# Layer-norm moments taken in the stage that writes the tile, and the input loaded in four transfers

## The reference

```python
def _layernorm(x, axis=-1, eps=1e-05):
    m = jnp.mean(x, axis=axis, keepdims=True)
    v = jnp.var(x, axis=axis, keepdims=True)
    return (x - m) / jnp.sqrt(v + eps)
...
    x = x + _L0_attn_ref(_layernorm(x, axis=-1), ...)
    x = x + _L0_ffn_ref(_layernorm(x, axis=-1), ...)
    ...
    x = x + _L3_ffn_ref(_layernorm(x, axis=-1), ...)
    return x
```

## Time and profile before

| what | value |
|---|---|
| median of 3 runs | 4477.09 us (4474.5 to 4481.69) |
| the profiled execution's own time | 4479.81 us |
| its span in the trace | 4478.1 us |
| TensorE (PE) busy | 3905.1 us, 87% |
| VectorE (DVE) busy | 2310.9 us, 52% |
| ScalarE (ACT) busy | 1725.0 us, 39% |
| GpSimd (POOL) busy | 1224.5 us, 27% |
| mean granted TensorE clock | 0.921 |

### The profile page before, as it was taken

One profiled execution on the slowest core, in us unless ns is written; L12 is line 12 of the kernel. 1 busy time (PEld: TensorE's weight loads), 2 busy tenths in 40 slices (PEclk: granted clock), 3 DMA queues, 4 the chain that ended last, 5 costly groups with the idle time before them and its releaser, 6 DMA issues. The chain is left out here.

```text
span 4478.1 us, 105382 instructions
## 1 busy us (share of the span) xinstructions
PE 3905.1 (87%) x45357; PEld 2429.4 (54%) x45424; DVE 2310.9 (52%) x4298; ACT 1725.0 (39%) x2719; POOL 1224.5 (27%) x1771
## 2 busy tenths in 40 slices
PE   7887759999995685799899779999999999999869
PEld 3333555555543373477555545656666666666636
DVE  5764243444555124344433256776677776766541
ACT  2345222112112010455211145666556665555532
POOL 2000120000003314311000035555555555554511
PEclk9999759999996797899899889999999999999879
DMA  1000000000003062100100000000000000000000
GB/s 51 1 1 1 30 0 26 11 2 10 11 3 111 26 195 62 40 1 1 57 1 0 8 8 9 9 11 11 9 10 9 9 9 9 9 9 9 6 15 19
DMA packets 38396, 92.00 MB, mean 21 GB/s; under 512 B 7422, under 2 KB 27679, under 8 KB 34426
## 3 DMA queue, kind: packets, MB, share of 16 engines
q1 hardware_dynamic: 27578, 69.54, 4.6%
q0 software_dynamic: 6144, 11.62, 0.9%
q10 hardware_dynamic: 4224, 4.19, 0.3%
HBM read 70.05 MB, written 20.45 MB: 20 GB/s over the span
## 5 line engine op out<-in xcount | busy, mean ns | idle before, releaser
L2725 PE MATMUL ps<-h_normT,h_w 128*128 128x512 f32 (+1 forms) x1008 | 425.0, 526 | 28.7 <-DVE h_xx L3312 21.6
L3246 DVE SCALAR_TENSOR_TENSOR h_cv<-h_raw,h_cw,h_cv 128x1023 f32<-128x1023 f32 (+2 forms) x288 | 389.2, 1361 | 20.0 <-ACT h_cv L3073 18.9
L3390 DVE SCALAR_TENSOR_TENSOR h_st<-h_st,d_gcs,ps 128x64 f32<-128x64 f32 x448 | 123.5, 276 | 345.7 <-PE ps L3021 345.6
L3072 ACT ACTIVATE h_raw<-ps 128x512 f32<-128x512 f32 x192 | 114.2, 595 | 404.1 <-PE ps L2725 403.3
L2725 PEld LDWEIGHTS ps<-h_normT,h_w 128*128 128x128 f32 x1008 | 165.3, 190 | 134.3 <-issue 116.8
L472 ACT ACTIVATE a_prob<-ps 128x1024 f32<-128x1024 f32 (+1 forms) x192 | 154.6, 811 | 192.8 <-PE ps L384 104.6
L956 PE MATMUL ps<-a_probT,a_v 128*128 128x512 f32 x512 | 227.6, 603 | 0.8 <-DVE a_probT L1094 0.8
L2622 POOL TENSOR_TENSOR h_gm<-h_gm,h_tmp 128x15 f32<-128x15 f32 (+7 forms) x480 | 217.3, 453 | 37.6
L2187 PE MATMUL ps<-h_normT,e_wgu 128*128 128x512 f32 (+1 forms) x448 | 204.1, 599 | 5.2 <-DMA e_wd<-in_e_wd 4.0
L1243 POOL MEMSET r_zero<- 128x2048 f32 x1 | 1.8, 1807 | 728.2 <-POOLq L54 728.2
L3021 PEld LDWEIGHTS ps<-h_st,h_mT 64*64 64x64 f32 x1792 | 90.7, 133 | 199.1 <-issue 195.0
(11 more groups left out here) (537 smaller groups left out, 9336.6 us busy)
## 6 DMA issues: line engine op xcount, KB each, us to landing
m_wgu<-in_m_wgu SPq DMA_DIRECT2D x8, 1408.0 KB
h_w<-in_d_w SPq DMA_DIRECT2D x48, 128.0 KB
m_wd<-in_m_wd SPq DMA_DIRECT2D x8, 704.0 KB
m_rows_in<-r_zero SPq DMA_DIRECT2D x4, 1024.0 KB
e_xe<-m_rows_in SPq DMA_DIRECT2D x8, 512.0 KB
m_rows_out<-e_y ACTq DMA_DIRECT2D x8, 512.0 KB
e_wgu<-in_e_wgu SPq DMA_DIRECT2D x1, 3520.0 KB
a_t_raw<-in_t_w SPq DMA_DIRECT2D x4, 768.0 KB
```

Source lines behind the costliest of these rows:

```text
L2725: last = pe.matmul(ps[:, PROJ[m], lo:hi], w[:, kind, k, :], hT[:, k, b * S + tb * BANK + lo:b * S + tb * BANK + hi], start=(k == 0), stop= ...
L3246: dve.scalar_tensor_tensor(out=d, in0=raw[:, kind, 0:S - back], scalar=tap(pr, kind, TAPS3 - 1 - back), in1=d, op0=ALU.mult, op1=ALU.add). ...
```

## The change

`core` gets a stats tile that lives for the whole run. `bn_stats` leaves `layer_norm`, which starts with the 16 `bn_aggr`. Each stage that adds the last term of a tile runs `bn_stats` (the helper `measure`) on that tile: as a rule one step behind, that is after the next tile's add has been issued, behind a wait for the tile's own add, and for the last tile (or the last two) after the loop. For x as loaded, `bn_stats` runs in `load_and_constants`, where VectorE measures four tiles behind each of four transfers of 512 KB; SyncE no longer waits there. In `add_rows` the add of r = 0 gets the wait for the add before it, too. In `thought0` the scaled adds get a semaphore, and the first half is measured between `moments_own(1)` and `finish(1)`.

```diff
+        self.stats = sb("x_stats", [P, NT, 6])
+def measure(core, dve, t):
+    return dve.bn_stats(core.stats[:, t, :], core.x[:, t, :])
...load_and_constants
-            sp.dma_start(core.x[:], core.dram["x"]).then_inc(loaded, 16)
-            sp.wait_ge(loaded, 16)
+            for i in range(PIECES):
+                t0, t1 = piece(i).start, piece(i).stop
+                sp.dma_start(core.x[:, t0:t1, :], core.dram["x"][:, t0:t1, :]).then_inc(loaded[i], 16)
+        @block.vector
+        def _(dve):
+            for i in range(PIECES):
+                dve.wait_ge(loaded[i], 16)
+                for t in piece(i):
+                    measure(core, dve, t)
...layer_norm
-            for t in range(NT):
-                dve.bn_stats(stats[:, t, :], core.x[:, t, :]).then_inc(stats_ready, 1)
             for t in range(NT):
-                dve.wait_ge(stats_ready, t + 1)
-                dve.bn_aggr(mv[:, t, :], stats[:, t, :]).then_inc(mv_ready, 1)
+                dve.bn_aggr(mv[:, t, :], core.stats[:, t, :]).then_inc(mv_ready, 1)
...attention0 (experts2 the same)
                 dve.tensor_tensor(core.x[:, t, :], ps[:, t % 8, 0:H], core.x[:, t, :], ALU.add).then_inc(x_added, 1)
+                if t >= 1:
+                    dve.wait_ge(x_added, t)
+                    measure(core, dve, t - 1)
+            dve.wait_ge(x_added, NT)
+            measure(core, dve, NT - 1)
...thought0
-                                             op0=ALU.mult, op1=ALU.add)
+                                             op0=ALU.mult, op1=ALU.add).then_inc(x_done, 1)
             moments_own(1)
+            for n in range(HALF):
+                dve.wait_ge(x_done, n + 1)
+                measure(core, dve, n)
             finish(1)
+            for n in range(HALF, NT):
+                dve.wait_ge(x_done, n + 1)
+                measure(core, dve, n)
...attention1
                 dve.tensor_tensor(xs, ps[:, u % 4, :].rearrange("p (t n) -> p t n", t=2), xs, ALU.add).then_inc(x_added, 1)
+                if u >= 1:
+                    dve.wait_ge(x_added, u)
+                    measure(core, dve, 2 * u - 2)
+                    measure(core, dve, 2 * u - 1)
+            dve.wait_ge(x_added, NT // 2)
+            measure(core, dve, NT - 2)
+            measure(core, dve, NT - 1)
...combine1, add_rows
-                    if r >= 1:
+                    if n >= 1:
                         dve.wait_ge(added, n)
-                    elif t >= NT // 2:
+                    if r == 0 and t >= NT // 2:
                         dve.wait_ge(x_added, t - NT // 2 + 1)
                     dve.scalar_tensor_tensor(...).then_inc(added, 1)
+                    if r == 0 and t >= 1:
+                        measure(core, dve, t - 1)
+            dve.wait_ge(added, NT * TOP1)
+            measure(core, dve, NT - 1)
...scan_mlp2
             def residuals(i):
+                if i >= 3:
+                    dve.wait_ge(x_added, i - 1)
+                    measure(core, dve, order[i - 3])
                 dve.wait_ge(out_p, i)
...
+            dve.wait_ge(x_added, NT + 1)
+            measure(core, dve, order[NT - 2])
+            measure(core, dve, order[NT - 1])
...heads3
             def end(t):
                 for g in range(2):
                     gate(t, g)
+                dve.wait_ge(xa, 4 * UNITS3)
                 for k in range(4):
                     add(t, k)
+                    for j in range(2):
+                        measure(core, dve, 2 * k + j)
+                    if k >= 1:
+                        dve.wait_ge(xa, 4 * UNITS3 + k)
+                        for j in range(2):
+                            measure(core, dve, NQ + 2 * k - 2 + j)
+                dve.wait_ge(xa, 4 * UNITS3 + 4)
+                for j in range(2):
+                    measure(core, dve, NT - 2 + j)
```

More of the change, by code:

```diff
@@ L71, in load_and_constants @@
     with Phase(core, "init") as ph:
-        loaded, filled, shaped = ph.sem("loaded"), ph.sem("filled"), ph.sem("shaped")
+        filled, shaped = ph.sem("filled"), ph.sem("shaped")
+        PIECES = 4
+        loaded = [ph.sem(f"loaded{i}") for i in range(PIECES)]
         block = ph.block()
+        piece = lambda i: range(i * NT // PIECES, (i + 1) * NT // PIECES)
         @block.sync
         def _(sp):
-            sp.dma_start(core.x[:], core.dram["x"]).then_inc(loaded, 16)
-            sp.wait_ge(loaded, 16)
+            for i in range(PIECES):
[7 more added lines that the diff above has]
+                    measure(core, dve, t)
         @block.gpsimd
@@ L107, in layer_norm @@
     with Phase(core, tag) as ph:
-        stats = ph.sb("stats", [P, NT, 6])
         mv = ph.sb("mean_var", [P, NT, 2])
@@ L111, in layer_norm @@
         rstd = ph.sb("rstd", [P, NT])
-        stats_ready, mv_ready, std_ready, rstd_ready = (ph.sem(n) for n in ("stats", "mv", "std", "rstd"))
+        mv_ready, std_ready, rstd_ready = (ph.sem(n) for n in ("mv", "std", "rstd"))
         h_ready, turned, copied = ph.sem("h"), ph.sem("turned"), ph.sem("copied")
@@ L662, in thought0 @@
         (load, g_done, gated, summed, squared, var_sum, std_ready, t_ready, lin, a_ready, gelu, dlin, rep_ready, bc_done,
-         bc_ready, dve_own, pool_own, o_ready, stat, aggr, so_ready, norm, load_first, sig, biased) = (ph.sem(n) for n in (
+         bc_ready, dve_own, pool_own, o_ready, stat, aggr, so_ready, norm, load_first, sig, biased, x_done) = (ph.sem(n) for n in (
              "load", "g_done", "gated", "summed", "squared", "var_sum", "std", "t", "lin", "a", "gelu", "dlin", "rep", "bc_done",
-             "bc", "dve", "pool", "o", "stat", "aggr", "so", "norm", "load_first", "sig", "biased"))
+             "bc", "dve", "pool", "o", "stat", "aggr", "so", "norm", "load_first", "sig", "biased", "x_done"))
         block = ph.block()
```

## The result

The changed kernel takes 4460.7 us (median of 10 runs, 4447.2 to 4475.1) against 4477.1 of the kernel before (10 runs, 4472.8 to 4488.5). The ratio is 0.996, 95% interval 0.9947 to 0.9974: 16.4 us faster, 12 to 24 by the interval. The forecast was 4451.8.

A forecast was written before the change was run, and what follows sets the result against it. TensorE, busy 87% of 4478.1 us, was taken to idle at eight layer-norm starts awaiting the moments, 42.0 us in all. Eight edge gains sum to 25.3 us, taking the median from 4477.1 to 4451.8; range 4445 to 4461.

The forecast's parts named there:

- The removed group: At the start of all eight layer norms: 16 bn_stats, 5.25 us each time with other engines waiting, 42.0 us in all.
- the table: ScalarE's square-root table load in six of eight layer norms becomes late next, costing about 0.1 us each.
- The load: Input in four transfers: only the last quarter's four bn_stats exposed, 1.39 us; gain 3.8 us.
- Rival A: First 10 us: each quarter of the load pays its own landing in turn, 8.4 us lost, time 4460.2; 5%.
- attention0, mixer, experts2: Edges after these stages: VectorE idles enough to hide all but the last two measures; gain 4.5 us each.
- thought0 and attention1: Edges where VectorE has no gap: all 16 measures come back in full; gains 0 and -0.1 us.
- combine1: Edge after combine1: 15 measures hide in waits and the sixteenth too; gain 5.2 us, or 4.7 if wrong.
- heads3: Edge after heads3: add 2 is 0.25 us late, 2.25 us exposed in all; gain 2.9 us.
- Rival B: TensorE's clock in the layer norms' transposes: 3.7 us more gained (4448.1), 10%, or 5.9 lost (4457.7), 5%.
- C: Moments hide almost nowhere: attention0, combine1, mixer and experts2 give back all 16, 6.6 us remain, time 4470.5; 4%.
- D: Measures behind waits hold VectorE some 0.6 us each, exposed at all 129: 35 us slower, 4512; 1%.

The follow-up runs named there:

- e5: The changed kernel unaltered, measured again in a second session beside the kernel before: 4451.9 us against 4477.6.
- e8: Changed kernel with eight input transfers, the mixer's doubled measure gone, heads3's first sequence measured ahead of the gates: 4448.6 us, ratio to before 0.9938.
- e6: The changed kernel with the load as one transfer instead of four: 4454.9 us.
- e12: The changed kernel with every moved bn_stats issued twice, the first into a spare tile: 4418.5 us against 4423.9 of the kernel before.
- e1: The kernel before with the persistent stats tile allocated but unused: 4435.5 us against 4434.7, ratio 0.9995.
- e11: Changed kernel, still four transfers, the mixer's doubled measure gone, heads3's first sequence measured ahead of the gates: 4396.1 us against 4423.9 of the kernel before.
- e10: The changed kernel cut to load, layer norms 4 and 5, mixer, experts2 and store: 748.6 us against 754.5 of the kernel before cut likewise.

## Why the prediction was right, and where it was not

**The forecast** of 25.3 us stands as a sum of mechanisms: 26.8 by the edges of one profile, 25.7 in e5's session. The first session's 16.4 us just stay in the range (4460.7 against an upper end of 4461), and its interval does not hold 25.3. That 4460.7 stayed inside is luck, and so is e5's median, 0.1 us from the forecast, with runs of one kernel that far apart. The range was drawn from unknown costs at the edges; what it should have been drawn from is the scatter of the kernel itself. The kernel before spreads over 31 us in 18 runs of one session, and I had seen three of its runs within 7 us and took 0.2% for what a measurement can tell. That is the weakest step of the prediction.

**The removed group**, 5.25 us at each edge, and **the table** as what is late next: 12.14 - 10.89 = 1.25 us from the first `bn_aggr` to the square root instead of 1.18; 0.1 was counted, 0.07 to 0.08 found at the six edges with a load.

**The load**: right in kind, 0.5 us too low. I took the last quarter's landing as what decides. In fact the first quarter's does: it landed at 4.82, and from there 16 measures fill VectorE without a pause to 10.15, so later quarters are never waited for. Rival A, a load broken by its pieces, did not come for four pieces; with eight (e8) VectorE did wait piece by piece, at a price of 1.1 us and not 8.4. The rule of the Trainium skill quoted in the prediction ("DMA: Bandwidth & Descriptors", section Measured (HBM→SBUF, 128 partitions, SWDGE, issued from GpSimd)) asks for transfers of at least 1 MiB. It is a rule for bandwidth, and followed here with one transfer it would have cost this edge its 4.1 us: e6 is the measurement that decides, while e8 bears out the direction of its warning.

**attention0, mixer, experts2**: right within 0.05 us. VectorE's idle time before each add shrank by the measure's 0.33 us at attention0 and experts2 (1.30 to 0.97, 5.62 to 5.29), and the adds kept their distance; the last two measures are what is exposed.

**thought0 and attention1**: the moved work came back in full; attention1 exactly, thought0 but for 0.5 us, since the gap before the layer norm shrank from 1.24 to 0.88.

**combine1**: the last measure hid; the gap fell from 3.75 to 3.12 us while the layer norm's first instruction came 4.06 us after the start of the last add, where it had come after 4.24. Its first `bn_aggr` was thus at least as early as if there were no measure. Which engine holds that barrier the rows do not show.

**heads3**: add 2 was 0.21 us late (1.92 after add 1 instead of 1.71), forecast 0.25. I charged the tail 0.3 us too much, as the gap behind VectorE's end fell from 1.84 to 1.59: a part of it was hidden there, too.

**Rival B** of the prediction, the clock in the transposes: their sum was 44.7 us, 0.9 less than before, and between 44.1 and 47.7 in six other profiles with the change. The pause before them did shrink (9.7 to 5.2 us at attention0, 9.1 to 4.6 at experts2), but no steady gain came from it. **Rivals C and D** are out by the table, which has the four hiding stages at their forecast, and by e12: even two measures per tile stay hidden where one is.

## What to carry to other kernels

Work that a barrier-bound phase begins with is worth moving into the stage before only where the moved engine idles there: read its idle time ahead of the last operations, and count in full what it has no gap for, and what stands behind the last one. A quantity like the moments, which is a function of one finished tile, is a good candidate. Input in a few pieces paid here, where the 16 measures take 5.3 us and the data about as long; too many pieces gave 1.1 us of it back. Before a range is given, look at how far runs of the same kernel lie apart, and judge a change of half a percent by its edges in the trace and not by the total alone.

## What was not expected of the hardware

- The scatter of this kernel goes mostly with TensorE's granted clock inside heads3. Among its small matrix products with short pauses between, the clock changes between its two levels: from 67 to 150 us of a stretch of about 1535 ran at 1.2 GHz in twelve profiles, and the stretch took from 1518 to 1550 us. Why it differs from one execution to the next is not shown.
- The kernel before took 4477 and 4478 us in two sessions and 4435 and 4424 in two others. The stage of 32 experts holds the 42 us between the first and e1's session: from the first tile of h in layer norm 3 to the first instruction of layer norm 4, e1's profile has 369.9 us and that of before 415.5, with the same work. The place can be narrowed. TensorE's waits in that stage of before begin with this row (us in total, times, longest), where "issue" stands for idle time with no wait that the profile shows:

```profile
PE ps L1179 <- issue: 44.8, 13, 15.2
```

These are products of the shared expert that come singly there and in one row in e1, where the profile has no such idle time in the stage:

```profile
1482.01 0.58 PE L1179 MATMUL ps<-m_sd,r_hid 128*128 128x256 f32 x1 [2.24 <-issue]
...
1457.31 12.00 PE L1180 MATMUL ps<-m_sd,r_hid 128*128 128x256 f32 x48 [1.40 <-DVE r_hid L1384]
```

With the gate products of the same expert it is 46 to 55 us in before, after and e5 to e8, and nothing in e1, e11 and e12. So it comes with the session and not with the change; what holds TensorE up there was not tried.
- With four pieces of the input the first quarter landed at 4.6 to 4.9 us in the whole kernel and at 5.2 in e10; with eight pieces the first landed at 3.96, and the fifth was waited for until 8.58.
